# A four-layer graph network: attention over halves of 1568 destinations in place of 1600, score search over 3136 sources in place of 3200, convolutions over 3125 columns in place of 3200

## The chip, the core and the metric

The kernel runs on one core of one Trainium2 chip. The metric is the device time of one launch in microseconds (us). PE is TensorE, DVE is VectorE, ACT is ScalarE, POOL is GpSimd, SP is SyncE; PEld is the load of a matmul's stationary operand.

## What is computed

A graph has 3125 nodes of 128 features and 100000 edges. Four layers follow one another, each added to its input: a softmax-weighted sum over edges, two graph attention (GAT) passes, three graph convolutions (GCN) with a batch norm, and a sum by 16 edge types. The change touches the two middle ones:

```
# GAT, twice:                                  # GCN, three times:
h = (x @ W).reshape(n, H, C)                   xl = h @ W[l]
e = leaky_relu(a_src[src] + a_dst[dst], 0.2)   agg = segment_sum(norm * xl[src], dst) + b[l]
m = segment_max(e, dst)                        hr = agg (+ h_last)
ex = exp(e - m[dst])                           hn = (hr - mean) * rsqrt(var + EPS) * gamma + beta
alpha = ex / segment_sum(ex, dst)[dst]         h = relu(hn)
out = segment_sum(alpha * h[src], dst) + bias
```

## The kernel before

The edges are turned once into two dense matrices in device memory, `ac_dram`: for each tile of 128 source nodes (25 tiles, `NT`, padded to `NPAD` = 3200 nodes) and each of 3200 destinations, the summed edge weight and the number of edges. After that both middle layers are dense.

A GAT pass (`gat_layer`, four heads, run twice) has three blocks. The first projects the features and makes the two scores of each node. The second finds the largest score over the sources of each destination. For each of 25 tiles `T` of destinations and each head, DVE runs one max over a row of 3200 sources with a mask added (line 1359, `row` and `mask`, written to `dump` or `acc`), 100 of them a pass. In the first pass DVE also makes a 0/1 tile (`there`, line 1339), PE transposes it in five steps (line 1307) and ACT turns it into the mask (line 1327), which is also kept in memory; the second pass loads the masks. Beside it PE counts degrees with one-column matmuls (line 1311) on columns that SP loads.

The third block (`gat_sums`) works in four parts, of two halves of the destinations (`HALF` = 1600) times two pairs of heads. A part has 50 units, one for each tile of sources and each head of the pair. A unit has four steps over all destinations of the half: on DVE the score `z` = max(steep + a, flat) (line 1507, `peak`), on ACT the exponential (line 1470), on DVE the product with the edge counts `count` (line 1546), and on PE four matmuls of `PIECE` = HALF/4 = 400 columns that add into four banks of PSUM (line 1612). DVE runs `peak` two units ahead; `z` has four buffers, `p` three, `count` two, each loaded by SP for one pair of units (line 1425). The two heads of a pair write the lower and upper 64 rows of PSUM. Ahead of a part `steep` and `flat` are made by 32 matmuls (lines 1583 and 1584, `lift`) and 16 copies on ACT (line 1437, `lay`); for the first part of a pass nothing covers them, for the others they are spread between units 24 and 44 of the part before. What follows a part (divide, bias, the bend of the elu, the transposes back to `hT`, lines 1443 to 1601) lies between the units of the next part, and stands alone only behind the last one.

Every float32 matmul of the program appears in the trace as two records, each with its own weight load.

The three GCN layers (`gcn_layer`) project 25 tiles, then add 25 strips: for each tile of sources a strip of 128 x 3200 weights comes from memory (five buffers, line 1713), and PE runs seven matmuls on it with the same stationary tile `xl` (line 1727), six of 512 columns and one of the rest, all seven into PSUM. Then DVE alone scales, adds the bias, makes the statistics and normalizes, in operations over all 3200 columns (lines 1744 to 1757), and the next layer begins.

Semaphores set all order; the instruction streams are written out by hand.

Of the kernel before, what the change touches and what calls it, by code (L numbers as in the profile page):

```python
# [8 lines left out]
ALU = mybir.AluOpType  # L9
# [4 lines left out]
N_NODES, D = 3125, 128  # L14
N_EDGES = 100000
NT = -(-N_NODES // P)
NPAD = NT * P
# [21 lines left out]
BIG = 2.0 ** 100  # L39
# [1125 lines left out]
            step(v.tensor_tensor(m.x[:, :, :], m.x[:, :, :], sums, ALU.add))  # L1165


HALF = NPAD // 2
PIECE = HALF // 4
FLOOR = 3e38  # L1170


def gat_layer(nc, m, weight, att_src, att_dst, bias, first):

    blocks = [slice(k * 512, min(k * 512 + 512, NPAD)) for k in range(7)]
    acc, acc2, h = (r.rearrange("p t f -> p (t f)") for r in (m.acc[:, :, :], m.acc2[:, :, :], m.h[:, :, :]))
    with phase(nc) as (sb0, ps0, sem0, block0):
# [67 lines left out]
        with phase(nc) as (sb, ps, sem, block_):  # L1245
            row = sb("row", [P, HEADS, NPAD])
            mask = [sb("mask0", [P, NPAD], BF16), sb("mask1", [P, NPAD], BF16)]
            dump = [acc[:, 0:NPAD], sb("dump", [P, NPAD])[:, :]]
# [81 lines left out]
            @block.vector  # L1330
            def _(dve):
                v = nc.vector

                def mark(T):

                    dve.wait_ge(col_in[T % 2], 16 * (T // 2 + 1))
                    if T >= 2:
                        dve.wait_ge(turned, STEPS * (T - 1))
                    v.tensor_scalar(there[:, T % 2, :], cols_of[T % 2].rearrange("p t d -> p (t d)"), 1.0, None, ALU.min).then_inc(marked, 1)

                v.memset(ones[:, :], 1.0)
                v.memset(minus[:, :], -BIG)
                v.tensor_copy(ident_b[:, :], m.ident[:, :]).then_inc(ready, 1)
                dve.wait_ge(ready, 1)
                if first:
                    mark(0)
                for T in range(NT):
                    if first:
                        if T + 1 < NT:
                            mark(T + 1)  # L1350
                        dve.wait_ge(masked, STEPS * (T + 1))
                    else:
                        dve.wait_ge(mask_in[T % 2], 16 * (T // 2 + 1))
                    for k in range(HEADS):
                        if T == 0:
                            dve.wait_ge(taken, 7 * (k + 1))
                        if T * HEADS + k >= 2:
                            dve.wait_ge(topped, T * HEADS + k - 1)
                        v.tensor_tensor_reduce(dump[k % 2], row[:, k, :], mask[T % 2][:, :], 1.0, -BIG, ALU.add, ALU.max,  # L1359
                                               top[:, T, k:k + 1]).then_inc(topped, 1)  # L1360
                dve.wait_ge(topped, HEADS * NT)
                step = Chain(dve, d_)
                step(v.tensor_tensor(top[:, :, :], top[:, :, :], a_dst[:, :, :], ALU.add))
                step(v.scalar_tensor_tensor(top[:, :, :], top[:, :, :], 0.2, top[:, :, :], ALU.mult, ALU.max))
                dve.wait_ge(counted, NT)
                step(v.tensor_scalar(into[:, :], sums[:, 0:NT], -1.0 if first else 0.0, None, ALU.add))
        gat_sums(nc, m, hw, a_src, b_row, top, att_rep, hwT)


UNITS = 2 * NT  # L1370
BLOCKS = -(-HALF // P)


def gat_sums(nc, m, hw, a_src, b_row, top, att_rep, hwT):
# [4 lines left out]
    acc, acc2, h_ = (r.rearrange("p t f -> p (t f)") for r in (m.acc[:, :, :], m.acc2[:, :, :], m.h[:, :, :]))  # L1379
    with phase(nc) as (sb, ps, sem, block_):  # L1380
        steep, flat = sb("steep", [P, 2, 2, HALF]), sb("flat", [P, 2, 2, HALF])
        count = sb("count", [P, 2, HALF])
        minus, diag = sb("minus", [P, P]), sb("diag", [P, BLOCKS, P])
# [1 line left out]
        both = shared[:, :, :].rearrange("p b n -> p (b n)")  # L1385
        y, tail = (both[:, k * BLOCKS * 2 * HC:(k + 1) * BLOCKS * 2 * HC] for k in range(2))
        share = sb("share", [P, BLOCKS, 2])
        z = [h_[:, 0:HALF], h_[:, HALF:], acc[:, 0:HALF], acc[:, HALF:2 * HALF]]
        p = [acc2[:, 0:HALF], acc2[:, HALF:2 * HALF], sb("p", [P, HALF])[:, :]]
        saved = sb("saved", [P, HALF])[:, :]  # L1390
        body = saved[:, 0:BLOCKS * 2 * HC]
# [296 lines left out]
def gcn_layer(nc, m, l, weight, b, gamma, beta):  # L1688

    with phase(nc) as (sb, ps, sem, block_):  # L1690
        w, xl = sb("w", [P, D]), sb("xl", [P, NT, D])
        strip = sb("strip", [P, STRIPS, NPAD])
        par = sb("par", [P, 3])
        pieces = [(s, min(s + 512, N_NODES)) for s in range(0, N_NODES, 512)]
        stats, mv = sb("stats", [P, len(pieces), 6]), sb("mv", [P, 2])
        scale, shift = sb("scale", [P, 1]), sb("shift", [P, 1])
        total = ps("total", [P, 8 * 512])
        w_in, p_in, done, taken, used, d_, var_ready, root = (
            sem(n) for n in ("w_in", "p_in", "done", "taken", "used", "d", "var_ready", "root"))
        strip_in = [sem(f"strip_in{k}") for k in range(STRIPS)]  # L1700
        block = block_()
        blocks = [slice(k * 512, min(k * 512 + 512, NPAD)) for k in range(7)]

        @block.sync
        def _(sp):
            sp.dma_start(w[:, :], weight).then_inc(w_in, 16)
            with nc.allow_non_contiguous_dma(reason="a number a partition"):
                for k, v in enumerate((b, gamma, beta)):
                    sp.dma_start(par[:, k:k + 1], v.unsqueeze(1)).then_inc(p_in, 16)
            for t in range(NT):  # L1710
                if t >= STRIPS:
                    sp.wait_ge(used, t - STRIPS + 1)
                sp.dma_start(strip[:, t % STRIPS, :], m.ac_dram[t][:, 0, :]).then_inc(strip_in[t % STRIPS], 16)

        @block.tensor
        def _(pe):
            pe.wait_ge(w_in, 16)
            for t in range(NT):
                if t >= 4:
                    pe.wait_ge(taken, t - 3)  # L1720
                nc.tensor.matmul(total[:, t % 4 * 512:t % 4 * 512 + D], m.hT[:, t * P:(t + 1) * P], w[:, :], start=True, stop=True).then_inc(done, 1)
            pe.wait_ge(taken, NT)
            for t in range(NT):
                pe.wait_ge(strip_in[t % STRIPS], 16 * (t // STRIPS + 1))
                into = strip[:, t % STRIPS, :]
                for cols in blocks:
                    last = nc.tensor.matmul(total[:, cols], xl[:, t, :], into[:, cols], start=t == 0, stop=t == NT - 1)  # L1727
                last.then_inc(used, 1)

        @block.scalar  # L1730
        def _(act):
            for t in range(NT):
                act.wait_ge(done, t + 1)
                nc.scalar.activation(xl[:, t, :], total[:, t % 4 * 512:t % 4 * 512 + D], ACT.Copy, scale=m.dinv[:, t:t + 1]).then_inc(taken, 1)  # L1734
            act.wait_ge(var_ready, 1)
            nc.scalar.activation(scale[:, :], scale[:, :], ACT.Sqrt).then_inc(root, 1)

        @block.vector
        def _(dve):
            v = nc.vector  # L1740
            step = Chain(dve, d_)
            dve.wait_ge(p_in, 48)
            dve.wait_ge(used, NT)
            step(v.tensor_tensor(m.hT[:, :], total[:, 0:NPAD], m.dinv_row[:, :], ALU.mult))
            if l == 0:
                step(v.tensor_scalar(m.lastT[:, :], m.hT[:, :], par[:, 0:1], None, ALU.add))
            else:
                step(v.scalar_tensor_tensor(m.lastT[:, :], m.hT[:, :], par[:, 0:1], m.lastT[:, :], ALU.add, ALU.add))
            for k, (s, e) in enumerate(pieces):
                step(v.bn_stats(stats[:, k, :], m.lastT[:, s:e]))  # L1750
            step(v.bn_aggr(mv[:, :], stats[:, :, :].rearrange("p k s -> p (k s)")))
            v.tensor_scalar(scale[:, :], mv[:, 1:2], EPS, None, ALU.add).then_inc(var_ready, 1)
            dve.wait_ge(root, 1)
            step(v.reciprocal(scale[:, :], scale[:, :]))
            step(v.tensor_tensor(scale[:, :], scale[:, :], par[:, 1:2], ALU.mult))
            step(v.tensor_scalar(m.hT[:, :], m.lastT[:, :], mv[:, 0:1], scale[:, 0:1], ALU.subtract, ALU.mult))
            step(v.tensor_scalar(m.hT[:, :], m.hT[:, :], par[:, 2:3], 0.0, ALU.add, ALU.max))


def rgcn_table(nc, m, rel_weights):  # L1760
# [177 lines left out]
```

## Time and profile before

| | us |
|---|---|
| median of 3 runs | 6825.32 |
| lowest and highest | 6819.9, 6832.18 |
| the profiled execution, its time | 6829.46 |
| its span, first to last instruction | 6828.0 |
| GAT, second and third blocks, pass 1 | 2781 to 3169, 3169 to 3933 |
| the same, pass 2 | 3982 to 4315, 4315 to 5083 |
| GCN, the three layers | 5138 to 5626 |

Busy shares over the span: PE 73%, DVE 68%, POOL 38%, ACT 24%. The shares are means over stages with different limits, so they are read by stage. What lies ahead of 2727 us (sorting edges, the dense matrices, layer 0) and behind 5664 us (the sum by edge types) has none of the changed code.

### The profile page before, as it was taken

What the parts mean: (1) busy time and instruction counts of PE and PEld (TensorE: products, weight loads), DVE (VectorE), ACT (ScalarE), POOL (GpSimd) and SP (SyncE); (2) the same over time, 40 slices, a digit from 0 to 9 for tenths busy, and PEclk for the clock granted to TensorE, in tenths of its full rate; (3) what the DMA queues carried; (4) which work ended last, traced back from release to release, by engine and by line L of the source; (5) the groups of instructions that cost most, each with busy time, mean ns of one, the idle gap of its engine ahead of it and who ended that gap; (6) DMA issues with size and microseconds to landing.
All of it is one profiled execution on the core that took longest, in us unless ns stands there. A gap on an engine that the chain in (4) does not pass through costs nothing. (4 is left out here: it accounts for less than half of the span.)

```text
span 6828.0 us, 71514 instructions
## 1 busy us (share of the span) xinstructions
PE 4951.0 (73%) x19096; PEld 3093.0 (45%) x19096; DVE 4675.9 (68%) x6628; ACT 1634.4 (24%) x3088; POOL 2614.4 (38%) x2433
## 2 busy tenths in 40 slices
PE   2777774258888886997888897788868886555555
PEld 1255553235555554785333277333324443333333
DVE  7699999957777776798999989899981101111112
ACT  0044442023333200323455410355530003000000
POOL 0177777778888885000000000000000000777774
PEclk9999999999999998656999965899999998555555
DMA  2000002434343311453333356233326666222221
GB/s 78 7 8 8 8 8 58 113 107 135 124 133 128 109 43 35 141 159 101 113 114 111 106 155 186 89 113 113 112 76 241 241 241 165 53 53 53 53 53 45
DMA packets 427374, 681.15 MB, mean 100 GB/s; under 512 B 86757, under 2 KB 308611, under 8 KB 417355
## 3 DMA queue, kind: packets, MB, share of 16 engines
q1 hardware_dynamic: 349282, 569.41, 25.9%
q0 software_dynamic: 77808, 107.93, 6.4%
q8 instruction: 181, 2.97, 0.2%
q14 instruction: 103, 0.84, 0.0%
HBM read 536.29 MB, written 140.87 MB: 99 GB/s over the span
## 5 line engine op out<-in xcount | busy, mean ns | idle before, releaser
L1043 POOL DMA_INDIRECT ring<-rel_dram,rel_col x782 | 744.4, 952 | 3345.7 <-SPq L71 3107.6
L954 PE MATMUL total<-to,from 128*128 128x256 f32 x2816 | 857.6, 420 | 228.5 <-issue 140.8
L790 POOL DMA_INDIRECT cells_dram<-rec,place x816 | 830.1, 1017 | 451.9 <-issue 242.7
L1077 PE MATMUL total<-ring,onehot 128*128 x1612 | 541.5, 498 | 455.7 <-DMA ring<-rel_dram,rel_col 452.0
L1612 PE MATMUL sums<-acc,hw 128*64 128x400 f32 x2144 | 759.5, 510 | 140.2 <-DVE acc L1546 139.7
L848 POOL DMA_INDIRECT ring<-l_dram,src_pair x600 | 758.0, 1263 | 182.9 <-issue 182.9
L1054 DVE TENSOR_SCALAR onehot<-iota,loc_pair 128x128 f32<-128x128 f32 x806 | 177.2, 286 | 816.9 <-PE total L1077 816.9
L954 PEld LDWEIGHTS total<-to,from 128*128 128x128 f32 x2816 | 467.1, 195 | 573.0 <-issue 545.8
L1077 PEld LDWEIGHTS total<-ring,onehot 128*128 128x128 f32 x1612 | 402.8, 310 | 594.8 <-issue 532.7
L1612 PEld LDWEIGHTS sums<-acc,hw 128*64 128x64 f32 x2144 | 269.1, 138 | 596.0 <-issue 316.5
L545 PE MATMUL node<-moved,onehot 128*128 128x75 f32 x1584 | 365.8, 426 | 221.6 <-DVE moved L419 221.6
L545 PEld LDWEIGHTS node<-moved,onehot 128*128 128x128 f32 x1584 | 345.3, 330 | 247.8 <-DVE moved L419 247.4
L1612 PE MATMUL sums<-p,hw 128*64 128x400 f32 x1056 | 383.2, 506 | 62.9 <-DVE p L1546 62.7
L887 DVE TENSOR_TENSOR to<-iota,rec 128x1024 f32<-128x1024 f32 x176 | 215.9, 1227 | 295.8 <-PE total L954 293.3
L1470 ACT ACTIVATE acc<-acc,a_src 128x1600 f32<-128x1600 f32 x200 | 325.8, 1629 | 359.7 <-DVE acc L1507 359.7
L1470 ACT ACTIVATE h<-h,a_src 128x1600 f32<-128x1600 f32 x200 | 325.6, 1629 | 359.3 <-DVE h L1507 359.3
L1727 PE MATMUL total<-strip,xl 128*128 128x512 f32 (+1 forms) x1050 | 403.8, 547 | 1.6 <-ACT xl L1734 1.6
L1507 DVE SCALAR_TENSOR_TENSOR h<-steep,a_src,flat 128x1600 f32<-128x1600 f32 x200 | 374.6, 1873 | 41.9 <-ACT steep L1437 41.9
L875 ACT ACTIVATE stage<-total 128x1280 f32<-128x1280 f32 x125 | 154.7, 1237 | 1027.4 <-PE total L954 1024.9
L508 ACT ACTIVATE same<-alike,unit 128x128 bf16<-128x128 f32 x800 | 281.5, 377 | 440.9 <-DVE below L408 436.2
L1507 DVE SCALAR_TENSOR_TENSOR acc<-steep,a_src,flat 128x1600 f32<-128x1600 f32 x200 | 374.4, 1872 | 0.0
L1359 DVE CUSTOM_DVE_ANT_0 acc<-row,mask 128x3200 f32<-128x3200 f32 x100 | 348.5, 3485 | 23.0 <-ACT mask L1327 11.7
(389 smaller groups left out, 8038.8 us busy)
## 6 DMA issues: line engine op xcount, KB each, us to landing
count<-ac_dram SPq DMA_DIRECT2D x200, 800.0 KB, 4.3
strip<-ac_dram SPq DMA_DIRECT2D x75, 1600.0 KB, 7.1
ac_dram<-stage SPq DMA_DIRECT2D x125, 640.0 KB, 3.5
h<-ac_dram SPq DMA_DIRECT2D x26, 1600.0 KB, 8.0
acc<-ac_dram SPq DMA_DIRECT2D x24, 1600.0 KB, 8.4
lo_row<-lo_dram SPq DMA_DIRECT2D x102, 256.0 KB, 3.5
rel_dram<-rows SPq DMA_DIRECT2D x25, 1024.0 KB, 5.4
mask_dram<-mask SPq DMA_DIRECT2D x25, 800.0 KB, 5.0
```

The source lines that it names most:

```text
L508: nc.scalar.activation(same[:, b, u, :], alike[:, b, u, :], ACT.Relu, bias=unit[:, 0:1], scale=1 / (2 * BIG), accum_out=mates[:, b, u:u + 1])
L545: last = nc.tensor.matmul(psum[:, b, u, 0:3 * NT], onehot[:, b, u, :], moved[:, b, u, :], start=True, stop=True)
L790: pool.indirect_dma_start(m.cells_dram[:, :], bass.IndirectOffsetOnAxis(ap=m.place[:, j:j + 1], axis=0), m.rec[:, j, :], None, bounds_chec ...
L848: pool.indirect_dma_start(fetched_row(j), None, m.l0_dram[:, :], bass.IndirectOffsetOnAxis(ap=m.src_pair[:, j:j + 1], axis=0)).then_inc(fe ...
L954: nc.tensor.matmul(spots[:, at(spot), :].rearrange("p o n -> p (o n)"), from_[:, n % 2, u, :], to[:, n % 2, u, :, :].rearrange("p k d -> p ...
L1043: pool.indirect_dma_start(ring[:, c % SLOTS, :], None, m.rel_dram[:, :], bass.IndirectOffsetOnAxis(ap=m.rel_col[:, c:c + 1], axis=0)).then ...
L1077: last = nc.tensor.matmul(total[:, at(col, D)], onehot[:, j % U, :], rows, start=False, stop=False, skip_group_check=True)
L1359: v.tensor_tensor_reduce(dump[k % 2], row[:, k, :], mask[T % 2][:, :], 1.0, -BIG, ALU.add, ALU.max, top[:, T, k:k + 1]).then_inc(topped, 1)
L1470: nc.scalar.activation(z[n % 4], z[n % 4], ACT.Exp, bias=a_src[:, 1, t, k:k + 1]).then_inc(exped, 1)
L1507: v.scalar_tensor_tensor(z[n % 4], steep[:, i % 2, kk, :], a_src[:, 0, t, k:k + 1], flat[:, i % 2, kk, :], ALU.add, ALU.max).then_inc(peak ...
L1612: last = nc.tensor.matmul(psum[kk * 2 * HC:(kk + 1) * 2 * HC, banks(i) + q, 0:PIECE], hw[:, t, k, :], p[n % 3][:, piece], start=t == 0, st ...
L1727: last = nc.tensor.matmul(total[:, cols], xl[:, t, :], into[:, cols], start=t == 0, stop=t == NT - 1)
```

## The change

`HALF` becomes the smallest multiple of 32 that covers the 3125 nodes with two halves, 1568, so `PIECE` becomes 392. `BLOCKS`, the number of 128-blocks in a half, stays 13. The max over sources reads 3136 of 3200. In the GCN the seventh matmul of a strip has 53 columns in place of 128, and five lines of DVE work on 3125 columns. No instruction is added, removed or moved: each engine issues the same list, with other sizes. The strips and the columns that are loaded for the degrees keep their size.

```diff
-HALF = NPAD // 2
+HALF = -(-N_NODES // 64) * 32
 PIECE = HALF // 4
...
-                        v.tensor_tensor_reduce(dump[k % 2], row[:, k, :], mask[T % 2][:, :], 1.0, -BIG, ALU.add, ALU.max,
+                        v.tensor_tensor_reduce(dump[k % 2][:, 0:2 * HALF], row[:, k, 0:2 * HALF], mask[T % 2][:, 0:2 * HALF], 1.0, -BIG, ALU.add, ALU.max,
                                                top[:, T, k:k + 1]).then_inc(topped, 1)
...
-        z = [h_[:, 0:HALF], h_[:, HALF:], acc[:, 0:HALF], acc[:, HALF:2 * HALF]]
+        z = [h_[:, 0:HALF], h_[:, HALF:2 * HALF], acc[:, 0:HALF], acc[:, HALF:2 * HALF]]
...
-        blocks = [slice(k * 512, min(k * 512 + 512, NPAD)) for k in range(7)]
+        blocks = [slice(k * 512, min(k * 512 + 512, N_NODES)) for k in range(7)]
+        hT, lastT = m.hT[:, 0:N_NODES], m.lastT[:, 0:N_NODES]
...
-            step(v.tensor_tensor(m.hT[:, :], total[:, 0:NPAD], m.dinv_row[:, :], ALU.mult))
+            step(v.tensor_tensor(hT, total[:, 0:N_NODES], m.dinv_row[:, 0:N_NODES], ALU.mult))
             if l == 0:
-                step(v.tensor_scalar(m.lastT[:, :], m.hT[:, :], par[:, 0:1], None, ALU.add))
+                step(v.tensor_scalar(lastT, hT, par[:, 0:1], None, ALU.add))
             else:
-                step(v.scalar_tensor_tensor(m.lastT[:, :], m.hT[:, :], par[:, 0:1], m.lastT[:, :], ALU.add, ALU.add))
+                step(v.scalar_tensor_tensor(lastT, hT, par[:, 0:1], lastT, ALU.add, ALU.add))
...
-            step(v.tensor_scalar(m.hT[:, :], m.lastT[:, :], mv[:, 0:1], scale[:, 0:1], ALU.subtract, ALU.mult))
-            step(v.tensor_scalar(m.hT[:, :], m.hT[:, :], par[:, 2:3], 0.0, ALU.add, ALU.max))
+            step(v.tensor_scalar(hT, lastT, mv[:, 0:1], scale[:, 0:1], ALU.subtract, ALU.mult))
+            step(v.tensor_scalar(hT, hT, par[:, 2:3], 0.0, ALU.add, ALU.max))
```

## Rows read from the trace of the kernel before

**Rows 1.** Windows of 100 us: PE, PEld, DVE, ACT, POOL busy, PEclk, DMA share, GB/s
```profile
2900.00:3000.00 100.00, 90.53 (x483) 85.36 (x483) 100.00 (x60) 22.53 (x30) 0.00 (x0) 0.50 0.52 151
3500.00:3600.00 100.00, 89.42 (x278) 34.77 (x274) 100.00 (x59) 50.33 (x41) 0.00 (x0) 1.00 0.35 115
4200.00:4300.00 100.00, 75.80 (x350) 75.20 (x350) 100.00 (x59) 0.00 (x0) 0.00 (x0) 0.50 0.57 157
5500.00:5600.00 100.00, 100.00 (x263) 46.67 (x262) 0.00 (x0) 0.00 (x0) 0.00 (x0) 1.00 0.74 270
```
**Rows 2.** Groups by line and form: busy us, mean ns | idle before, releaser
```profile
L1359 DVE CUSTOM_DVE_ANT_0 dump<-row,mask 128x3200 f32<-128x3200 f32 x100 | 348.5, 3485 | 1.9 <-ACT row L1318 1.9
L1507 DVE SCALAR_TENSOR_TENSOR h<-steep,a_src,flat 128x1600 f32<-128x1600 f32 x200 | 374.6, 1873 | 41.9 <-ACT steep L1437 41.9
...
L1546 DVE SCALAR_TENSOR_TENSOR acc<-h,count 128x1600 f32<-128x1600 f32 x134 | 243.0, 1813 | 0.0
```
**Rows 3.** Source line 1748: duration ns min/median/max
```profile
L1748 DVE SCALAR_TENSOR_TENSOR lastT<-hT,par,lastT x2: 3552/3552/3552, 5448.8 to 5612.7; 128x3200 f32<-128x3200 f32 x2
```
**Rows 4.** Timeline, max over sources, pass 1: start, us, what, [idle before]
```profile
3003.91 10.77 PE L1311 MATMUL sums<-ones,acc 128*128 128x1 f32 x50
...
3010.22 3.48 DVE L1359 CUSTOM_DVE_ANT_0 dump<-row,mask 128x3200 f32<-128x3200 f32 x1
...
3013.64 1.82 DVE L1339 TENSOR_SCALAR there<-h 128x3200 bf16<-128x3200 f32 x1
...
3015.51 1.25 PE L1307 MATMUL turn<-ident_b,there 128*128 128x128 bf16 x10 [0.82 <-DVE there L1339]
```
**Rows 5.** Timeline, one unit of `gat_sums`, pass 1
```profile
3607.17 1.87 DVE L1507 SCALAR_TENSOR_TENSOR acc<-steep,a_src,flat 128x1600 f32<-128x1600 f32 x1
...
3610.70 1.87 DVE L1507 SCALAR_TENSOR_TENSOR h<-steep,a_src,flat 128x1600 f32<-128x1600 f32 x1
...
3610.82 2.90 PE L1612 MATMUL sums<-p,hw 128*64 128x400 f32 x8 [0.63 <-DVE p L1546]
```
**Rows 6.** Timeline, the stretch with `lift` between units
```profile
3298.45 1.88 DVE L1507 SCALAR_TENSOR_TENSOR acc<-steep,a_src,flat 128x1600 f32<-128x1600 f32 x1
...
3305.51 1.88 DVE L1507 SCALAR_TENSOR_TENSOR h<-steep,a_src,flat 128x1600 f32<-128x1600 f32 x1
```
**Rows 7.** Timeline, start of `gat_sums` in pass 2
```profile
4323.19 0.83 PE L1583 MATMUL sums<-hwT,att_rep 128*128 128x400 f32 x2
...
4323.86 0.83 PE L1584 MATMUL sums<-diag,minus 128*128 128x400 f32 x2
...
4341.78 1.88 DVE L1507 SCALAR_TENSOR_TENSOR h<-steep,a_src,flat 128x1600 f32<-128x1600 f32 x1 [8.86 <-ACT steep L1437]
```
**Rows 8.** Source line 1425: the loads of `count`
```profile
DMA to landing us min/median/max: 4.1/4.3/5.8
```
**Rows 9.** Groups by line and form: the strip matmuls of the GCN
```profile
L1727 PE MATMUL total<-strip,xl 128*128 128x512 f32 x900 | 399.0, 593 | 1.6 <-ACT xl L1734 1.6
...
L1727 PE MATMUL total<-strip,xl 128*128 128x128 f32 x150 | 28.8, 274 | 0.0
```
**Rows 10.** Timeline, weight loads at the end of one strip
```profile
5276.90 0.41 PEld L1727 LDWEIGHTS total<-strip,xl 128*128 128x128 f32 x3 [0.24 <-issue]
...
5277.12 0.19 PEld L1727 LDWEIGHTS total<-strip,xl 128*128 128x128 f32 x1
5277.56 0.19 PEld L1727 LDWEIGHTS total<-strip,xl 128*128 128x128 f32 x1 [0.24 <-issue]
```
**Rows 11.** Windows of 1 us, line 1311 alone: PE, PEld busy, PEclk, DMA
```profile
3983.30:3984.30 1.00, 1.00 (x11) 1.00 (x10) 1.00 0.00 0
...
3986.30:3987.30 1.00, 1.00 (x6) 1.00 (x6) 0.50 0.05 16
```
**Rows 12.** Timeline, DVE behind the strips of GCN layer 1
```profile
5282.77 3.49 DVE L1744 TENSOR_TENSOR hT<-total,dinv_row 128x3200 f32<-128x3200 f32 x1 [152.25 <-PE total L1727]
5286.30 1.89 DVE L1746 TENSOR_SCALAR lastT<-hT,par 128x3200 f32<-128x3200 f32 x1
```

## The prediction

> **What bounds the kernel now.** First the windows, since the changed code lies in three kinds of stages with different limits. In the max over sources DVE is busy 100 us of 100 in both passes, while PE at the lower level of its clock (granted clock 0.50, 1.2 GHz) is at 90.5 and 75.8; in `gat_sums` DVE is again at 100 of 100, PE at 89.4 with its clock at 2.4 GHz, ACT at 50; in the GCN DVE is at 0 and PE at 100 [rows 1]. So two stages are DVE's and one is PE's. Second the groups of DVE's three large lines: the idle time before them is 1.9, 41.9 and 0.0 us in all, so nothing but their own length sets their pace, and the 41.9 us is the wait for `steep` at the start of the two passes [rows 2]. Third the timelines, for what stands behind DVE and how near it is. They come with the steps below.
>
> **The max over sources (line 1359).** 200 instructions lose 64 of 3200 columns. What a column costs is read from one operation at two lengths: 3552 ns for 3200 columns [rows 3] and 1873 ns for 1600 [rows 2], so 1679 ns for 1600, 1.05 ns a column; what is left over is fixed and stays. 200 x 64 x 1.05 = 13.4 us. If the whole duration scaled, 3485/3200 = 1.09 ns, it would be 13.9. The cover: in pass 1 a tile of destinations lasts some 15.5 us (four maxima of 3.42, from 3010.22 to 3013.64, and 1.82 for `there`), PE's count for it starts at 3003.91 and ends at 3014.7, and PE then waits 0.82 us for DVE's `there` [rows 4]. DVE becomes 4 x 0.067 = 0.27 us faster a tile, PE's work does not shrink, so PE's wait becomes some 0.55 us and PE stays second. The degree loads keep their size; in pass 2 PE is busy only 76 of 100 us [rows 1]. All 13.4 us reach the end.
>
> **The units of `gat_sums` (lines 1507 and 1546).** There are 400 units with one `peak` and one product each, each 32 columns shorter: 800 x 32 x 1.05 = 26.9 us. By the whole durations, 1873/1600 and 1813/1600 [rows 2], it would be at most 29.5. A unit starts every 3.53 us (3607.17 to 3610.70). In it PE needs 2.90 us for its eight records and waits 0.63 us for `p` [rows 5]; it shrinks along, by 8 x 8 columns of 0.83 ns, 0.05 us (the price of a column is worked out below), against 0.067 for DVE, so the wait hardly moves. In the stretches where `lift` adds its matmuls to the units two units still take 3298.45 to 3305.51, 7.06 us, as elsewhere [rows 6]; the 96 units there count in full. ACT is at half. The loads of `count` land in 4.1 to 5.8 us [rows 8], ahead of a pair of units that will take 6.93 in place of 7.06, and shrink by 2% as well.
>
> **Start and end of a pass.** At the start nothing covers `lift`: DVE waits 8.86 us before its second `peak` for the last copies to `steep` [rows 7], behind 64 records on PE, two of which take 4323.19 to 4323.86, 0.335 us each, for 400 columns: 0.83 ns a column. So 64 x 8 x 0.83 = 0.43 us a pass, 0.9 for both. The tail (copies of 1600 columns on ACT, narrower last transposes) gives about 0.1 us a pass by the same price of a column. Together 1.1 us.
>
> **The GCN on DVE.** Nothing runs beside it: line 1744 waited 152.25 us for PE, and PE waits for DVE afterwards. 75 columns fewer in each of twelve operations. Lines 1744 (three) and 1748 (two) run at one column a step: 5 x 75 x 1.05 = 0.39 us. Line 1746 (once) and lines 1756 and 1757 (three each) run at about twice that pace (1.89 us for 3200 columns beside 3.49 for line 1744 [rows 12]): 7 x 75 x 0.52 = 0.27 us. Together 0.7 us.
>
> **The GCN on PE: nothing, though it looks like the largest single cut.** The seventh matmul of a strip loses 75 of 128 columns, and PE is the bound here, with 1.6 us of idle time in 900 records [rows 9]. The slope of the two forms, (593 - 274)/384 = 0.83 ns a column, would make it 75 x 0.83 = 62 ns for each of 150 records, 9.3 us. But the step is not the duration. Weight loads start at 5276.90, then two more, the last at 5277.12, then 5277.56: a 128-column record takes a step of 0.11 us and a 512-column one 0.43 [rows 10]. Line 1311 shows what a record costs when it streams a single column behind the same 128x128 weight load: at 2.4 GHz 10 to 11 start in a microsecond, a step of 0.1 us, with the load row busy throughout [rows 11]. So 0.1 us is the floor that the weight load sets, the 128-column record already stands on it, and 53 columns (44 ns of stream) can't go below. The bounds are 0 and -9.3 us; I take 0, since rows 11 has the same load with still fewer columns. A cost of shortness is excluded by the same row.
>
> The Trainium skill has a rule that would give part of it: TensorE: Matmul & The Clock Gate, section Back-to-back issue gap, puts a warm record of 1 to 64 columns at about 60 cycles and one of 128 at 134. By that table, an estimate, 74 cycles at 2.4 GHz would be saved on each of 150 records, 4.6 us. The same section warns that the table leaves the weight load out, and no row here shows such a step with a new weight load.
>
> **The sum.** 13.4 + 26.9 + 1.1 + 0.7 + 0 = 42.1 us. Against the profiled execution's own 6829.46 us that is 6787.4. That execution is 4.1 us above the median of the three runs, 6825.32, and the stages outside the change are the same in both, so against the median I forecast **6783 us**, 0.6% less. The three runs spread over 12.3 us, so 0.2% (13.7 us) is about what can be told from no change.
>
> **Rivals.**
>
> *Short matmuls pay off (0.07).* For it: the durations in rows 9 do follow the columns. Against it: rows 10 and 11. Full price 9.3 us more: 6774.
>
> *An odd length loses the fast pace (0.08).* 3125 is odd, and every operation of the trace that runs at two columns a step has an even length. Lines 1746, 1756 and 1757 would then take some 3.45 us in place of 1.9: 7 x 1.55 = 10.9 us lost: 6794. Nothing in the rows speaks for or against it, since no odd length occurs there. The Trainium skill, VectorE: DVE Perf Modes, section What auto-detection actually checks, keeps the pace where the outermost counts of source and destination are both even or equal. Here both are 3125, so by it the rival falls, and it stays a tenth at most.
>
> *Part of attention has another bound (0.04).* If PE set the pace in the 96 units with `lift`, where its queue holds three units' worth of work in two, their 96 x 0.067 = 6.4 us would be missing: 6789. The even spacing in rows 6 speaks against it.
>
> *Slower: PE's clock falls in the strip loops (0.02).* In the degree counts PE is busy without a gap, and yet its granted clock falls from 1.00 to 0.50 between two rows in which it does nothing but one-column records behind weight loads [rows 11], while `gat_sums` and the GCN hold 1.00 [rows 1]. The change brings records of that kind into the strips: in each, two stream for less time than their load takes. At 1.2 GHz a strip of 12 x 0.43 + 2 x 0.11 = 5.4 us would last 10.8. The gain is gone once 42/5.4, about 8, of 75 strips run so, and with all of them the time is 6783 + 405 = 7188. Against it: 5.2 of a strip's 5.4 us are full 512-column records as before, and `gat_sums` holds 1.00 though PE waits in every unit.
>
> **The numbers.** The forecast has 0.79, the others 0.07, 0.08, 0.04 and 0.02. The range takes in the first two rivals and the 6 us by which the runs lie off their median: 6766 to 6801. All but the clock rival end over 0.2% faster; with a little for a disturbed comparison that is 0.95 faster, 0.03 within 0.2%, 0.02 slower.
>
> **What would show it.** Line 1359 at 3418 ns, line 1507 at 1840 and line 1546 at 1780, DVE still at 100 of 100 in the windows and its idle time before line 1546 still 0. The first starts of line 1507 some 3.46 us apart. The GCN's strip loops as long as before, 134 us, with three weight loads inside 0.22 us for the short records, whose own duration falls to some 210 ns all the same: a busy time that goes down with no time gained. Lines 1746 and 1757 at 1.85 us; 3.4 would be the odd-length rival. I am wrong if a strip gets shorter, if PE's granted clock is below 1.00 in the strips, or if DVE gets idle time in attention.

## The result and the profile after

| | before | after |
|---|---|---|
| median, six runs each | 6826.75 us | 6783.1 us |
| lowest to highest | 6819.9 to 6832.18 | 6780.55 to 6785.02 |
| ratio of after to before, 95% interval | | 0.9936 [0.9923, 0.9949] |
| the profiled execution, its time | 6829.46 | 6782.41 |

The three-run median of before given above, 6825.32, became 6826.75 with three more runs. The change saves 43.7 us by the medians; 42.1 were forecast, and 6783 us.

The limits of the stages are as they were. Windows of after, 100 us each; the columns are those of [rows 1]:

```profile
2900.00:3000.00 100.00, 91.88 (x500) 85.94 (x500) 100.00 (x60) 26.28 (x35) 0.00 (x0) 0.50 0.60 172
3500.00:3600.00 100.00, 84.73 (x256) 31.61 (x254) 100.00 (x60) 51.31 (x40) 0.00 (x0) 1.00 0.36 117
...
5450.00:5550.00 100.00, 100.00 (x263) 46.66 (x262) 0.00 (x0) 0.00 (x0) 0.00 (x0) 1.00 0.80 292
```

DVE has no gap in these windows of attention, nor in one of the max in pass 2 (4150 to 4250 us, PE at 82 of 100); the granted clocks are the same, and the GCN's strips still belong to PE, at 1.00. So the time must have gone where DVE's starts moved together. Timeline of after, in the max over sources and in `gat_sums` (start, duration, instruction):

```profile
3001.28 3.46 DVE L1359 CUSTOM_DVE_ANT_0 dump<-row,mask 128x3136 f32<-128x3136 f32 x1
3004.62 1.86 DVE L1339 TENSOR_SCALAR there<-h 128x3200 bf16<-128x3200 f32 x1
...
3006.54 1.25 PE L1307 MATMUL turn<-ident_b,there 128*128 128x128 bf16 x10 [0.56 <-DVE there L1339]
```
```profile
3601.41 1.93 DVE L1507 SCALAR_TENSOR_TENSOR acc<-steep,a_src,flat 128x1568 f32<-128x1568 f32 x1
3603.18 1.87 DVE L1546 SCALAR_TENSOR_TENSOR acc<-h,count 128x1568 f32<-128x1568 f32 x1
3604.88 1.93 DVE L1507 SCALAR_TENSOR_TENSOR h<-steep,a_src,flat 128x1568 f32<-128x1568 f32 x1
```

A max starts 3.34 us before what follows it (3001.28 to 3004.62), where [rows 4] had 3.42. PE's wait for `there` went from 0.82 to 0.56 us, so PE is still second. A unit takes 3.47 us where [rows 5] had 3.53. Yet the rows themselves say something else. Groups of after, columns as in [rows 2]:

```profile
L1507 DVE SCALAR_TENSOR_TENSOR h<-steep,a_src,flat 128x1568 f32<-128x1568 f32 x200 | 381.2, 1906 | 40.8 <-ACT steep L1437 40.8
...
L1546 DVE SCALAR_TENSOR_TENSOR acc<-h,count 128x1568 f32<-128x1568 f32 x134 | 247.6, 1847 | 0.0
```

The mean of line 1507 rose from 1873 to 1906 ns and that of line 1546 from 1813 to 1847, with fewer columns and a faster pace; line 1359 went from 3485 to 3434, where 3418 were forecast. Such a duration runs past the start of the next instruction (1.93 us from 3601.41 ends at 3603.34, the next starts at 3603.18), so it isn't a step. What made it rise was not known at this point and is one of the questions of the experiments.

The other place to read is the GCN. Groups of after for the strips, and the weight loads at the end of a strip:

```profile
L1728 PE MATMUL total<-strip,xl 128*128 128x512 f32 x900 | 403.1, 598 | 1.6 <-ACT xl L1735 1.6
...
L1728 PE MATMUL total<-strip,xl 128*128 128x53 f32 x150 | 24.1, 242 | 0.0
```
```profile
5157.81 0.41 PEld L1728 LDWEIGHTS total<-strip,xl 128*128 128x128 f32 x3 [0.24 <-issue]
5158.46 0.19 PEld L1728 LDWEIGHTS total<-strip,xl 128*128 128x128 f32 x1 [0.24 <-issue]
```

The short form went from 274 ns [rows 9] to 242, and the long form from 593 to 598: what the two short records of a strip lost in length (2 x 32 ns) nearly all came back in the twelve long ones (12 x 5 ns). Taken one by one in the trace, it is a single one of each kind: the first of the two short records lasts 210 ns, the length that the forecast gave for both, the second is still 275, and the long record behind them grew from 595 to 657. The loads keep the pattern of [rows 10]: three of them within 0.22 us, 0.65 us from the first of the three to the one after the third. Behind the strips, in the first layer:

```profile
5242.29 1.85 DVE L1747 TENSOR_SCALAR lastT<-hT,par 128x3125 f32<-128x3125 f32 x1
```

DVE had waited 152.31 us for PE before line 1745 as against 152.25 [rows 12], and line 1747 takes 1.85 us with its odd length, so it kept the fast pace.

Here are the stages of both profiled executions, taken from the first starts of the lines named, in us:

| stage | before | after | difference |
|---|---|---|---|
| ahead of the changed code | 2727.0 | 2719.9 | -7.2 |
| on to the first max (unchanged code) | 54.3 | 57.3 | +3.0 |
| max over sources, first to last start of line 1359, pass 1 and 2 | 384.45, 344.31 | 376.92, 339.38 | -7.5, -4.9 |
| last max to first start of line 1507, pass 1 and 2 | 17.7, 16.9 | 16.7, 17.3 | -1.0, +0.4 |
| units, first to last start of line 1507, pass 1 and 2 | 727.85, 727.84 | 714.33, 714.36 | -13.5, -13.5 |
| one layer's strips, first matmul to DVE's start | 134.71 | 134.65 | -0.06 |
| behind the GCN | 1170.3 | 1167.5 | -2.8 |

### The profile page after: what moved, and what is told of

It reads as the page before. It is cut to its first block and busy times, and to the rows that moved or that the text cites. A ratio compares the mean times of both kernels' runs of the same rounds, so it can differ in the third digit from the quotient of the medians.

```text
span 6780.9 us, 71514 instructions
## 1 busy us (share of the span) xinstructions
PE 4932.4 (73%) x19096; PEld 3093.7 (46%) x19096; DVE 4635.9 (68%) x6628; ACT 1621.7 (24%) x3088; POOL 2604.7 (38%) x2433
## 5 line engine op out<-in xcount | busy, mean ns | idle before, releaser
L1612 PE MATMUL sums<-acc,hw 128*64 128x392 f32 x2144 | 743.4, 503 | 137.3 <-DVE acc L1546 136.9
L1612 PE MATMUL sums<-p,hw 128*64 128x392 f32 x1056 | 377.5, 500 | 62.2 <-DVE p L1546 61.9
L1507 DVE SCALAR_TENSOR_TENSOR h<-steep,a_src,flat 128x1568 f32<-128x1568 f32 x200 | 381.2, 1906 | 40.8 <-ACT steep L1437 40.8
L1470 ACT ACTIVATE acc<-acc,a_src 128x1568 f32<-128x1568 f32 x200 | 320.5, 1602 | 352.2 <-DVE acc L1507 352.2
L1470 ACT ACTIVATE h<-h,a_src 128x1568 f32<-128x1568 f32 x200 | 320.4, 1602 | 351.9 <-DVE h L1507 351.9
L1507 DVE SCALAR_TENSOR_TENSOR acc<-steep,a_src,flat 128x1568 f32<-128x1568 f32 x200 | 381.3, 1906 | 0.0
L1359 DVE CUSTOM_DVE_ANT_0 acc<-row,mask 128x3136 f32<-128x3136 f32 x100 | 343.3, 3433 | 25.0 <-ACT mask L1327 13.0
```

Source lines behind the costliest of these rows:

```text
L1359: v.tensor_tensor_reduce(dump[k % 2][:, 0:2 * HALF], row[:, k, 0:2 * HALF], mask[T % 2][:, 0:2 * HALF], 1.0, -BIG, ALU.add, ALU.max, top[: ...
L1470: nc.scalar.activation(z[n % 4], z[n % 4], ACT.Exp, bias=a_src[:, 1, t, k:k + 1]).then_inc(exped, 1)
L1507: v.scalar_tensor_tensor(z[n % 4], steep[:, i % 2, kk, :], a_src[:, 0, t, k:k + 1], flat[:, i % 2, kk, :], ALU.add, ALU.max).then_inc(peak ...
L1612: last = nc.tensor.matmul(psum[kk * 2 * HC:(kk + 1) * 2 * HC, banks(i) + q, 0:PIECE], hw[:, t, k, :], p[n % 3][:, piece], start=t == 0, st ...
```

## The experiments

Two theories were open for attention (DVE's columns set the pace everywhere, or PE bounds the units with `lift`), and two for the strips (a short float32 record stands on the floor of its weight load, or it costs its columns). The first three runs below and the first one with seven equal matmuls shared one chip, on which the kernel before took 8118.01 us (median of 31 runs). In the profiles of these four variants, code ahead of the first max that none of them touches took 3767 to 3811 us in place of 2727.0, and the end 1402 to 1411 in place of 1170. The stages between that a variant leaves alone are within a microsecond of those of before. What these runs show therefore rests on the stages.

**Units alone.**

```diff
-HALF = NPAD // 2
+HALF = -(-N_NODES // 64) * 32
...
-        z = [h_[:, 0:HALF], h_[:, HALF:], acc[:, 0:HALF], acc[:, HALF:2 * HALF]]
+        z = [h_[:, 0:HALF], h_[:, HALF:2 * HALF], acc[:, 0:HALF], acc[:, HALF:2 * HALF]]
```

> The kernel before with HALF = 1568 alone: the units of gat_sums change, the max over sources stays at 3200 columns and the GCN at 3200. If DVE's own length sets the pace, starts of line 1507 stand 3.46 us apart in place of 3.53 and the time falls by 26.9 + 1.1 = 28 us against before (ratio 0.9959). If PE bounds the 96 units with lift, it is 21.6 us. Rows of line 1507 last longer than before by some 33 ns (1906, as in the changed kernel) if that rise comes from the new half, 1840 if not.

8098.94 us against 8118.01, ratio 0.997 [0.9945, 0.9996]. The units took 714.5 us in both passes where before took 727.8, together 26.7 us less; the max (383.6 and 345.0) and the strips (134.71) stayed. The medians, 19 us apart with an interval from 3 to 45 us, can't tell the 28 us forecast from the 21.6 of the other theory; the units can: the pace is that of DVE's columns. The rows of line 1507 have 1840 ns at the median, as the price of a column wants it, at a pace of 3.465 us. So the new half does not make them longer.

**The max alone.**

```diff
-                        v.tensor_tensor_reduce(dump[k % 2], row[:, k, :], mask[T % 2][:, :], 1.0, -BIG, ALU.add, ALU.max,
+                        v.tensor_tensor_reduce(dump[k % 2][:, 0:3136], row[:, k, 0:3136], mask[T % 2][:, 0:3136], 1.0, -BIG, ALU.add, ALU.max,
...
+                step(v.tensor_scalar(top[:, :, :], top[:, :, :], -40.0, None, ALU.max))
```

> The kernel before with the max over 3136 of 3200 columns alone (and one small operation a pass that bounds the maxima of the padding nodes from below, some 0.3 us). If DVE bounds both passes: starts of line 1359 at 3.345 us in place of 3.412, 13.4 us less, ratio 0.9981. If PE or the loads bound part of it, DVE shows new idle time before lines 1359 or 1339 and the gain is below 10 us.

8093.09 us, ratio 0.9978 [0.9952, 1.0004], which tells nothing by itself. The starts of line 1359 went from 3.412 to 3.346 us, and the stages from 384.5 and 344.3 to 376.7 and 339.1: 12.9 us, 13.4 forecast. The units stayed at 727.8.

**The GCN alone.**

```diff
-HALF = -(-N_NODES // 64) * 32
+HALF = NPAD // 2
```

> The changed kernel with HALF back at 1600 and the max back at 3200: only the GCN's 53 and 3125 columns are left. By the weight-load floor the three waits of DVE for the strips stay at 447 us together and the time falls by 0.7 us, which can't be told from 0 (ratio 0.9999). By the durations of the matmuls (62 ns for each of 150 records) the waits are 437.5 us and the ratio 0.9985.

8115.41 us, ratio 0.9996 [0.9964, 1.0029]. The three waits of DVE for the strips (line 1745 for line 1728) came to 447.0 us, not 437.5. A layer's strips took 134.65 us.

**No seventh matmul, and one of a single column.** These two ran with the next two on one chip beside before at 6827.95 us.

```diff
-                for cols in blocks:
-                    last = nc.tensor.matmul(total[:, cols], xl[:, t, :], into[:, cols], start=t == 0, stop=t == NT - 1)
+                for cols in (blocks if t == 0 else blocks[:6]):
+                    last = nc.tensor.matmul(total[:, cols], xl[:, t, :], into[:, cols], start=t == 0, stop=t == NT - 1 or cols == blocks[6])
```

> The changed kernel without the seventh matmul for 24 of the 25 strips of a layer (the last 53 columns of the sums are left out there). By the floor two steps of 0.107 us go in each of 72 strips, 15.4 us, and DVE's three waits are 431.6 us in place of 447. If 53 columns cost only their stream (44 ns), it is 6.4 us, and the waits are 440.6.

A layer's strips took 129.35 us in place of 134.65: 5.30 less, and 24 strips times two steps of 0.107 us are 5.14; with 0.1105 us, the mean by which these two loads stand apart from the next in the changed kernel's trace, they are 5.30. Three layers give 15.9 us; the stream of 53 columns alone would have given 6.4. Median of two runs 6770.56 us, ratio 0.9911 [0.9881, 0.994]. DVE's waits were 429.4 us, somewhat below the 431.6 forecast: these sums hold the projections and a load of `w` too, and with the same GCN code they were 447.0 us in some executions and 444.6 in others. The strips alone, from their first matmul, don't vary.

```diff
+                for cols in blocks[:6]:
...
+                cols = blocks[6] if t == 0 else slice(3072, 3073)
+                last = nc.tensor.matmul(total[:, cols], xl[:, t, :], into[:, cols], start=t == 0, stop=True, skip_group_check=True)
```

> The changed kernel with the seventh matmul of a strip at one column in place of 53 for 24 of the 25 strips of a layer (the last 52 columns of the sums are left out there). By the weight-load floor DVE's three waits for the strips stay at 447 us. By the columns (52 x 0.83 = 43 ns for each of 144 records) they fall to 440.8.

6782.87 us, ratio 0.9935 [0.9912, 0.9957], and 134.61 us a layer in place of 134.65. The row got shorter once more:

```profile
L1730 PE MATMUL total<-strip,xl 128*128 128x1 f32 x144 | 20.0, 208 | 0.0
```

274, 242 and 208 ns for 128, 53 and 1 column, and 134.71, 134.65 and 134.61 us for the strips. The busy time follows the columns, the time doesn't. DVE's waits were 444.6 us here, which is the other level just named and no gain of the single column: the next run has 53 columns and 444.6 us as well.

These runs show a floor of 0.11 us for a record with a new 128-column stationary tile. That it is the load, and not some price of any record, was not tested by a run with another width; a row of before speaks for the load. At the start of a unit of `gat_sums` two loads of a 64-column tile come one behind the other:

```profile
3610.82 0.19 PEld L1612 LDWEIGHTS sums<-p,hw 128*64 128x64 f32 x2 [1.33 <-DVE p L1546]
```

One of them lasts 0.14 us, so the second starts some 0.05 us behind the first, half of what three loads of a 128-column tile show in [rows 10].

**Buffers 1600 apart, and PE kept at 400 columns.**

```diff
-PIECE = HALF // 4
+WIDTH = 1600
+PIECE = 392
...
-        z = [h_[:, 0:HALF], h_[:, HALF:2 * HALF], acc[:, 0:HALF], acc[:, HALF:2 * HALF]]
-        p = [acc2[:, 0:HALF], acc2[:, HALF:2 * HALF], sb("p", [P, HALF])[:, :]]
+        z = [h_[:, 0:HALF], h_[:, WIDTH:WIDTH + HALF], acc[:, 0:HALF], acc[:, WIDTH:WIDTH + HALF]]
+        p = [acc2[:, 0:WIDTH], acc2[:, WIDTH:2 * WIDTH], sb("p", [P, WIDTH])[:, :]]
```

> The changed kernel with the buffers of gat_sums (steep, flat, count, z, p, saved) 1600 columns apart as before, and 1568 used. Time as the changed kernel, starts of line 1507 3.464 us apart. If the new offsets of the halves make the rows of lines 1507 and 1546 longer (1906 and 1848 ns where 1840 and 1780 were expected), they return to 1840 and 1780 here; if it is the length of 1568, they stay.

6785.02 us, ratio 0.9935 [0.9912, 0.9958]; the units took 714.8 us a pass and line 1507 had 1835 ns. That alone would have pointed to the offsets. But the units-alone and one-column runs have the offsets of the changed kernel and also about 1840 (1849 in the second). So neither length nor offset is the cause.

The second variant sets `PIECE = 400` and clears the last 32 columns of the three `p`:

> As the run before it, with PE's matmuls and ACT's small copies of gat_sums still at 400 columns while DVE and the exponentials work on 1568 (the 32 extra columns of the products are zeros, so nothing of the result is left out). If DVE alone sets the pace, starts of line 1507 stay 3.464 us apart in all units and only the uncovered starts and tails come back, some 1.1 us. If PE bounds the units with lift, those show starts over 3.47 us apart and up to 6.4 us come back.

6784.84 us, ratio 0.9941 [0.9918, 0.9963]. The units took 715.0 us a pass, 0.2 more than with 392 columns at the same offsets. In a stretch with `lift`:

```profile
3288.36 1.86 DVE L1508 SCALAR_TENSOR_TENSOR acc<-steep,a_src,flat 128x1568 f32<-128x1568 f32 x1
...
3302.23 1.85 DVE L1508 SCALAR_TENSOR_TENSOR acc<-steep,a_src,flat 128x1568 f32<-128x1568 f32 x1
```

Four units in 13.87 us, 3.47 each, as everywhere. PE has room for two per cent more columns and DVE doesn't notice. How PE keeps up is seen in the same stretch. Two units and the matmuls of `lift` between them are 24 records, which at 0.335 us would take 8.0 us of the 6.93 that DVE leaves. But once PE is behind, the records of the two heads, which write different halves of PSUM's rows, run side by side:

```profile
3299.60 0.50 PE L1615 MATMUL sums<-p,hw 128*64 128x400 f32 x1
3299.66 0.50 PE L1615 MATMUL sums<-acc,hw 128*64 128x400 f32 x1
```

They start 0.06 us apart, the next such pair 0.33 us later, and the 16 records of two units take 4.30 us (from 3290.75) where two lots of 2.90 [rows 5] would be 5.8.

**Seven equal matmuls.** If the short record is paid at the floor anyway, its unused time can carry columns of the long ones.

```diff
-        blocks = [slice(k * 512, min(k * 512 + 512, N_NODES)) for k in range(7)]
+        blocks = [(slice(k * 512, k * 512 + EVEN), slice(k * EVEN, k * EVEN + EVEN)) for k in range(7)]
...
-                for cols in blocks:
-                    last = nc.tensor.matmul(total[:, cols], xl[:, t, :], into[:, cols], start=t == 0, stop=t == NT - 1)
+                for to, cols in blocks:
+                    last = nc.tensor.matmul(total[:, to], xl[:, t, :], into[:, cols], start=t == 0, stop=t == NT - 1)
```

with `EVEN` = 448, and line 1745 reads 448 of each 512 columns of `total`.

> The changed kernel with each strip in seven matmuls of 448 columns in place of six of 512 and one of 53. More columns are streamed (3136 for 3125), in as many records. If a record's step is the longer of its stream (0.833 ns a column) and the weight load (0.107 us), a strip takes 14 x 0.375 = 5.25 us in place of 12 x 0.428 + 2 x 0.107 = 5.36, so 75 strips save 8 us and DVE's three waits are 439 us in place of 447. If the short records had no floor, a strip would last as long as now or 0.02 us longer, and the waits stay at 447.

On the chip of the first group 8064.94 us, ratio 0.9942 [0.9923, 0.9962]; a layer's strips took 131.92 us and DVE's three waits were 436.2 us, 439 forecast (these sums vary by some 2 us, as said above). Once more, beside the changed kernel:

> The changed kernel with seven matmuls of 448 columns a strip, once more, beside the other two: strip loops of 131.9 us in place of 134.65, 8.2 us below the changed kernel, some 6775 us.

6774.22 us, ratio 0.9927 [0.9913, 0.9941], 131.92 us again: 3 x 2.73 = 8.2 us in the strips, as forecast. The medians of the session are 11.1 us apart; the part ahead of the changed code, equal in both, was 3.0 us shorter in this profile. Its weight loads come evenly:

```profile
5150.15 0.19 PEld L1729 LDWEIGHTS total<-strip,xl 128*128 128x128 f32 x1 [0.19 <-issue]
5150.52 0.19 PEld L1729 LDWEIGHTS total<-strip,xl 128*128 128x128 f32 x1 [0.18 <-issue]
```

**The changed kernel again, and the best version.**

> The changed kernel once more, beside the best version on one chip. Forecast from its stages: 42 us below the kernel before, ratio 0.9938. The first profile had the max of pass 2 1.3 us longer than the same code in later profiles, and rows of line 1507 of 1904 ns at a start-to-start of 3.464 us: if those are of that execution alone, this profile shows some 1845 ns and the same pace.

6785.29 us beside 6822.73 for before, ratio 0.9942 [0.9928, 0.9955]. Line 1507:

```profile
L1507 DVE SCALAR_TENSOR_TENSOR h<-steep,a_src,flat x200: 1747/1842/1853, 3175.8 to 5012.6; 128x1568 f32<-128x1568 f32 x100
```

1842 ns and a pace of 3.465, with the same code that had shown 1904 and 3.464. The longer rows belonged to that one execution. The longer max of pass 2, which the expectation put down to that execution too, did not go away: 339.4 us again (its cause is in the next section).

```diff
-HALF = -(-N_NODES // 64) * 32
+HALF = -(-N_NODES // 8) * 4
```

on top of the seven equal matmuls:

> The changed kernel with seven matmuls of 448 columns a strip, HALF at 1564 (the smallest multiple of 4 that covers 3125 with two halves) and the max over 3128 columns. By the steps: 8.2 us from the strips, 800 x 4 x 1.042 = 3.3 us from the units, 200 x 8 x 1.042 = 1.7 us from the max: 13.2 us below the changed kernel, some 6770 us and a ratio of 0.9917 to the kernel before. If pieces of 391 columns or a half of 1564 bring a cost of their own, starts of line 1507 stand over 3.455 us apart and the ratio is at or above 0.9925.

6769.03 us, ratio 0.9917 [0.9904, 0.9931] to the kernel before; 6770 were forecast. Units stood 3.456 us apart, 712.8 us a pass, and the starts of the max 3.337. It is 16.3 us below the changed kernel's median of the same session, where 13.2 were forecast. By the stages of the two profiles 8.2 us come from the strips, 3.3 from the units and 0.8 from the max (1.7 forecast; its steps have the forecast length, but the first maxima of each pass are set by something else, see below), 12.4 in all; the part ahead of the changed code, which is the same in both, was 3.1 us shorter in its profile.

## Why the prediction was right

**What bounds each stage**: right. DVE stayed at 100 of 100 in the windows of attention and PE in the strips; the experiments on single parts and the one with PE at 400 columns show it.

**The price of a column**: right. The forecast took 1.05 ns from two durations. By starts, 0.0665 us for two operations of 32 columns each (3.531 to 3.4645 us) are 1.04. Units: 26.9 us forecast, 27.0 and 26.7 measured. Max: 13.4 forecast, 12.5 in the changed kernel's profile and 12.9 alone. The forecast let all of it reach the end, and that step was a little off: the first maxima of a pass run as fast as PE and ACT make `row`. Timeline of after, the start of pass 2:

```profile
3943.26 3.42 DVE L1359 CUSTOM_DVE_ANT_0 acc<-row,mask 128x3136 f32<-128x3136 f32 x1 [10.10 <-DMA mask<-mask_dram]
...
3958.09 3.43 DVE L1359 CUSTOM_DVE_ANT_0 dump<-row,mask 128x3136 f32<-128x3136 f32 x1 [1.94 <-ACT row L1318]
```

Three intervals take 14.8 us here (3943.26 to 3958.09) and 13.3 in before (3969.79 to 3983.08), whose trace has waits of 1.00 and 1.87 us there. The 1.5 us are what pass 2 lacks (4.9 measured where its 99 intervals were due 6.6). Only 0.2 of them, three intervals at 0.067, are the faster DVE waiting for the same rows. The rest is PE's clock. `row` is made by the matmuls of line 1296, whose first one starts at 3959.28 in before and at 3932.87 in after. Windows of line 1296, before and then after (PE and PEld busy, PEclk, DMA share, GB/s):

```profile
3963.00:3964.00 1.00, 1.00 (x4) 0.52 (x3) 1.00 1.20 302
```
```profile
3937.00:3938.00 1.00, 1.00 (x2) 0.34 (x1) 0.50 1.21 290
```

The granted clock came back from 0.50 to 1.00 3.0 us behind that first matmul in before and 5.8 us behind it in after, and while it was low the loads stood 0.85 us apart in place of 0.43. So the fourth max started 25.2 us behind it in place of 23.8. The change is not the reason: with the same shorter max the clock came back after 3.0 us in the run with PE at 400 columns, and its pass 2 took 338.0 us, the full 6.3 less than before, while in all the runs where it came back after 5.5 to 6.1 us the pass took 339.1 to 339.5. The matmuls just ahead (line 1242, the last of them ended 0.9 us before) are the same in all these runs, and what moved the clock's return stays open. In pass 1 the first four intervals are not DVE's either, since its fifth max waits for the mask that ACT makes. So some 0.5 us of the 13.4 could never come back, and the forecast counted them. It had read the 1.9 us of idle time in [rows 2] as all there was before line 1359; that group is one half of the maxima, and the other half in before has 23.0 us:

```profile
L1359 DVE CUSTOM_DVE_ANT_0 acc<-row,mask 128x3200 f32<-128x3200 f32 x100 | 348.5, 3485 | 23.0 <-ACT mask L1327 11.7 <-DMA mask<-mask_dram 10.2 <-ACT row L1318 1.0
```

**Start and end of a pass**: 1.1 us forecast. The stretches between the last max and the first unit gave 0.6 (17.7 + 16.9 to 16.7 + 17.3), and in the other profiles with 1568 columns a half the same stretch lies between 16.6 and 18.6 us, so it isn't settled.

**The GCN on DVE**: 0.7 us forecast. From line 1745's start to the end of line 1758 the first layer took 14.95 us in place of 15.14, 0.2 a layer, 0.6 in all over the three.

**The GCN on PE**: right, and the part with most to lose. 0 forecast between 0 and 9.3; 0.2 measured (3 x 0.06). The reason held in the runs made for it: 1 column costs what 53 cost, leaving the matmul out saves two floors of 0.11 us, and equal shares save 8.2 us with more columns.

**The sum**: 42.1 us forecast; 43.7 by the first medians, 37.4 by the second (6822.73 to 6785.29). The changed stages of the two profiles give 40.3 without the stretches between them, and the table shows 10.0 us of the first pair's 47 in code that nothing touched, ahead and behind, against 3.0 the other way. So the agreement with 6783 to a tenth of a microsecond has luck in it; that with the stages has not. The range was given a little wider than its own terms: 6774 less 6 and 6794 plus 6 are 6768 and 6800.

**The rivals**: short matmuls pay off, no (134.61 at one column). By the rule of the Trainium skill (TensorE: Matmul & The Clock Gate, Back-to-back issue gap) an estimated 4.6 us would have come; 0.2 did. The odd length loses the fast pace, no: 1850 ns for 3125 columns where 3200 took 1886. By the rule of the Trainium skill (VectorE: DVE Perf Modes, What auto-detection actually checks) it keeps it, and the trace agrees. Another bound in attention, not in the units with `lift` (3.47 us apart there even with PE at 400 columns), though the first maxima of a pass have one. The clock in the strips stayed at 1.00.

**The signs**: line 1507 at 1840 ns, 1546 at 1780 and 1359 at 3418 were missed by the first profile (1906, 1847, 3434) and met by the second of the same code (1841, 1781, 3419). The 210 ns for the short strip records came for one of the two only.

## What to carry to other kernels

Cut padding where the bounding engine's start-to-start step scales with it: there every column was worth its full price (1.04 ns in each of 800 operations here), and can be added up beforehand to a few per cent. Where a matmul streams for less time than its weight load takes, as the 53 columns (44 ns) did behind a load of 110 ns, it stands at the floor: trimming it to one column gave nothing, dropping it gave 0.22 us a strip and filling it 0.11. So try a split into equal pieces in place of full ones and a rest. Read such a step from the starts of the weight loads. The durations mislead, and even the starts of the matmuls can: behind the first short record the second starts after 46 ns, and the time comes back in front of the record after it.

## What was not expected

Record durations lie about a change in two ways. On PE the short records shrank by 32 and then 34 ns without a gain, while a long record behind them grew. On DVE the rows of lines 1507 and 1546 were some 60 ns longer in one execution than in another of the same code (1904 and 1842 ns for line 1507), and those of line 1359 some 15 ns, at a pace equal to 0.001 us.

On one chip the kernel before took 8118.01 us in place of 6822 to 6828. By the profiles of its variants there, all of it lay ahead of and behind the dense middle layers. What made those parts slower was not looked into.
